# Gate signals of a fused GNN kernel given by a PE drain behind the last product instead of by the product

## The reference, cut to what matters

```python
def _lstm_last(seq, wih, whh, bih, bhh):
    ...
    def step(carry, x_t):
        h, c = carry
        g = x_t @ wih.T + h @ whh.T + b
        i, f, gg, o = jnp.split(g, 4, axis=-1)
        c = jax.nn.sigmoid(f) * c + jax.nn.sigmoid(i) * jnp.tanh(gg)
        h = jax.nn.sigmoid(o) * jnp.tanh(c)
        return ((h, c), None)
...
msgs = x[src].reshape(n, d, c)
aggr = _lstm_last(jnp.swapaxes(msgs, 0, 1), wih, whh, bih, bhh)
return aggr @ wl.T + bl + x @ wr.T
...
x = _layernorm(x + sage(relu(sage(x))))        # two layers of _sage_conv
h = jax.ops.segment_sum((x @ weight[rel])[src] * norm[:, None], dst, num_segments=512)
x = _layernorm(x + relu(h))
```

## Time and profile before

| | us |
|---|---|
| median of 3 executions | 535.96 |
| lowest and highest of them | 535.65, 536.25 |
| span of the profiled execution | 570.4 |
| busy in that span: PE | 485.2 (85%) |
| busy: PE weight loads (they overlap PE) | 349.4 (61%) |
| busy: DVE | 399.5 (70%) |
| busy: ACT | 325.8 (57%) |
| busy: POOL | 309.4 (54%) |

### The profile page before, as it was taken

One profiled execution on the slowest core, in us unless ns is written; L12 is line 12 of the kernel. 1 busy time (PEld: TensorE's weight loads), 2 busy tenths in 40 slices (PEclk: granted clock), 3 DMA queues, 4 the chain that ended last, 5 costly groups with the idle time before them and its releaser, 6 DMA issues.

```text
span 570.4 us, 9783 instructions
## 1 busy us (share of the span) xinstructions
PE 485.2 (85%) x3463; PEld 349.4 (61%) x3463; DVE 399.5 (70%) x1114; ACT 325.8 (57%) x832; POOL 309.4 (54%) x320
## 2 busy tenths in 40 slices
PE   8766998979897999778897888887899987978795
PEld 4644786757676785656666766775785543444343
DVE  5544887858676895557776776876787975757665
ACT  4734766737556674545565665655675664545543
POOL 6476565665546501676664566666204655656551
PEclk9997999979999999978989999999999999999899
DMA  5665665675646502665665456556202111111111
GB/s 191 204 188 168 180 192 159 177 195 161 175 125 197 166 11 93 187 180 161 172 169 148 134 163 183 167 169 181 77 1 79 48 38 38 42 38 41 39 42 29
DMA packets 28346, 72.85 MB, mean 128 GB/s; under 512 B 6795, under 2 KB 10691, under 8 KB 28298
## 3 DMA queue, kind: packets, MB, share of 16 engines
q0 software_dynamic: 20768, 64.77, 40.0%
q1 hardware_dynamic: 6442, 6.54, 4.0%
q10 hardware_dynamic: 1088, 0.92, 0.5%
HBM read 69.05 MB, written 3.16 MB: 127 GB/s over the span
## 4 chain that ended last, share of the span: by engine, by line
PE 39%; DVE 17%; ACT 16%; another core or an unknown queue 13%; issue 8%; DMA 6%; POOL 1%; DVEq 0%; ACTq 0%; POOLq 0%
PE gates L1254 18%; DMA edge_rows<-msg_table,msg_index 6%; PE gates L1247 5%; PE work L1254 4%; DVE msg_full L1090 3%; ACT act_if L601 3%; ACT h_hi L597 3%; DVE prod_fc L906 2%; DVE prod_ig L908 2%; ACT msg_full L750 2%; PE work L1247 2%; DVE h_full L877 2%; ACT act_o L619 2%; ACT tanh_c L593 2%
## 5 line engine op out<-in xcount | busy, mean ns | idle before, releaser
L524 POOL DMA_INDIRECT rows<-gate_table,src_steps x226 | 224.7, 994 | 165.1 <-issue 64.5
L1247 PE MATMUL gates<-ident,rows 128*128 128x128 f32 x686 | 99.5, 281 | 39.5 <-issue 20.8
L601 ACT ACTIVATE act_if<-gates 128x512 f32<-128x512 f32 x113 | 67.8, 600 | 104.1 <-remote 54.5
L539 POOL DMA_INDIRECT edge_rows<-msg_table,msg_index x76 | 75.5, 993 | 79.6 <-DMA msg_table<-table_sb 30.9
L1254 PE MATMUL gates<-h_hi,whh_hi 128*128 128x256 f16 x396 | 104.7, 283 | 13.1 <-ACT h_hi L597 6.6
L906 DVE TENSOR_TENSOR prod_fc<-act_if,cell 128x256 f32<-128x256 f32 x128 | 54.2, 424 | 81.3 <-issue 37.3
L1247 PEld LDWEIGHTS gates<-ident,rows 128*128 128x128 f32 x686 | 78.1, 144 | 52.1 <-issue 49.7
L1254 PE MATMUL gates<-h_hi,whh_lo 128*128 128x256 f16 x396 | 104.1, 281 | 0.0
L1254 PE MATMUL gates<-h_lo,whh_hi 128*128 128x256 f16 x396 | 88.1, 282 | 0.4 <-issue 0.4
L890 DVE TENSOR_TENSOR h_lo<-h_full,h_hi 128x256 f16<-128x256 f32 x128 | 54.2, 423 | 12.3 <-ACT h_hi L597 0.9
L1080 DVE TENSOR_SCALAR rows<-node_iota,dst_f 128x512 f16<-128x512 f16 x132 | 43.4, 365 | 26.8 <-ACT msg_full L750 25.7
(11 more groups left out here) (186 smaller groups left out, 800.5 us busy)
## 6 DMA issues: line engine op xcount, KB each, us to landing
rows<-gate_table,src_steps POOLq DMA_INDIRECT x226
gate_table<-rows SPq DMA_DIRECT2D x8, 256.0 KB
edge_rows<-msg_table,msg_index POOLq DMA_INDIRECT x76
code<-code_table SPq DMA_DIRECT2D x6, 160.0 KB
msg_table<-table_sb SPq DMA_DIRECT2D x4, 192.0 KB, 2.4
code<-code_table SPq DMA_DIRECT2D x5, 128.0 KB
whhT<-turned_whh SPq DMA_DIRECT2D x2, 256.0 KB
wihT<-turned_wih ACTq DMA_DIRECT2D x1, 256.0 KB, 2.9
```

Source lines behind the costliest of these rows:

```text
L524: pool.indirect_dma_start(rows[:, j * K + k, :], None, gate_table[l], bass.IndirectOffsetOnAxis(src_steps[:, t, k:k + 1], axis=0)).then_in ...
L539: pool.indirect_dma_start(edge_rows[:, c % 2, n, :], None, msg_rows, bass.IndirectOffsetOnAxis(msg_index[:, pool_first(c) + n:pool_first(c ...
L601: act.activation(act_if[:, h, :], gates[:, h, 0, :], ACT.Sigmoid, scale=1 / G_SCALE).then_inc(if_ready[h], 1)
L1247: pe.matmul(gate_place(t, h, gate)[:, k * P:(k + 1) * P], rows[:, j * K + 2 * h + k, gate * P:(gate + 1) * P], ident[:, :], is_transpose=True,
```

## The change

The method `then_inc` is taken off the last product of each group and put on a `pe.drain()` that is added behind it. The semaphores, their counts and those who wait for them stay as they were. `drain` is an instruction of PE's sequencer. All of it lies in `recurrent`; the first step of each layer (`first_gates`) and step 1 of the first layer (`picked_last`) keep their signals on the matmuls.

```diff
                     pe.wait_ge(h_lo_ready[h], split)
-                    products(t, h, BANKS[0], (hi,), h_lo, True).then_inc(gates0[h], 1)
+                    products(t, h, BANKS[0], (hi,), h_lo, True)
+                    pe.drain().then_inc(gates0[h], 1)
                     if apart(t):
                         products(t, h, (GATE_G,), (hi, lo), h_hi)
-                        products(t, h, (GATE_G,), (hi,), h_lo, True).then_inc(gates1[h], 1)
+                        products(t, h, (GATE_G,), (hi,), h_lo, True)
+                        pe.drain().then_inc(gates1[h], 1)
                         products(t, h, (GATE_O,), (hi, lo), h_hi)
-                        products(t, h, (GATE_O,), (hi,), h_lo, True).then_inc(gates_o[h], 1)
+                        products(t, h, (GATE_O,), (hi,), h_lo, True)
+                        pe.drain().then_inc(gates_o[h], 1)
                     else:
                         products(t, h, BANKS[1], (hi, lo), h_hi)
-                        products(t, h, BANKS[1], (hi,), h_lo, True).then_inc(gates1[h], 1)
+                        products(t, h, BANKS[1], (hi,), h_lo, True)
+                        pe.drain().then_inc(gates1[h], 1)
```

## The result

The changed kernel takes 580.68 us (median of 4 executions, 579.02 to 581.35), the kernel before 535.81 (535.04 to 536.25): a ratio of 1.0856, 95% interval 1.0815 to 1.0898, slower by 45 us.

What follows compares the result with a forecast made beforehand. PE's throughput was taken to bound an undisturbed step, going from 4.43 to 6.21 us. Over 58 steps that gave 103 us, plus 6 for five other steps, less 5: +104 on 535.96, 640 us, range 592 to 672.

Steps and rivals of the forecast that it cites:

- the two loops: In a step with six drains, PE's own work was put at 6.21 us, the loop of dependences at 5.38 us.
- the closing drain: PE's drain at the kernel's end, taken to end 0.32 us behind the start of PE's last matmul.
- 0.30 us for each drain: PE's loss at each drain: 0.27 us between products, and with the slower second matmul 0.30 us.
- the long waits add: ACT's long waits at PE's signals, 54.5 us in 20, were to stay on top of the drains' cost; chance 0.55.
- The rival that swallows the waits: Long waits pass while PE works through its drains: 591 to 614 us; chance 0.24, shared with a cheap restart.
- don't become late: POOL's gathers wait for `gates1[1]` and come later, but their slot is read that much later too; no cost.
- the 5 us taken off: Six steps with one-hot selections (t = 2, 12, 21, both layers) hide half 0's three stalls, about 0.9 us each.
- The dearer drain: Each drain costs 0.10 us more than its row says: +37 us, 677 us; chance 0.12.
- the cheap restart: Matmuls behind a drain are taken in at once, losing 0.21 us: 609 us; chance 0.24, shared with swallowed waits.
- the drain that holds nothing: A drain gives only its signal, each step later by 0.05 us: +3 us, 539 us; chance 0.03.
- The clock: PE's clock falls to 1.2 GHz in the gaps, a step takes 10.5 us: +354 us, about 890 us; chance 0.03.
- Faster by freed signals: The sequencer's signal avoids the products' late way and ACT's waits shrink, at most 20 us: 519 us; chance 0.01.

Runs made afterwards that it cites:

- the run with signals on the products: Changed kernel with its drains kept but the signals put back on the last products, as before the change: 586.0 us.
- the pair without gathers: Kernel before and changed kernel, each with only the first 20 of 226 gathers: 485.7 us and 581.86 us.
- the second profile: Kernel before, unchanged, in a second profiled execution: 536.69 us, with a span of 534.9 us.
- the first profile: Kernel before, unchanged, in the profiled execution that the prediction read: span 570.4 us, where plain executions took 535.81 us.

## Why the prediction was wrong

**Right: what bounds an undisturbed step, and that a drain holds PE.** 40 matmuls at 0.109 us, each drain holding all products behind it, and PE the longer of the two loops: all as worked out. An undisturbed step was forecast at 6.21 us and takes 6.05.

**Nearly right: the price of a drain.** Forecast 0.38 us from product to product and 0.03 for the slower second one, 0.30 in all. Measured 0.354, and 0.117 instead of 0.109 for the second, so 0.25. The restart of 0.06 us, taken from the restart behind a sequencer wait, was exact. The 0.32 us before it were not: they came from the closing drain. The matmul ahead of it carries a signal, and the run with signals on the products has 0.320 us too; that this is the whole reason isn't shown, since that matmul has another shape. The signal reaches ACT 0.33 us behind the product's start (413.36 against 413.03) instead of 0.31, where 0.05 us more was forecast. The second matmul's 0.03 us belongs to transposes of 32-bit rows (0.136 us behind the sixth drain), products pay 0.008. Behind the sixth drain I put 0.05 us for the sequencer's wait; it is 0.15 (0.502 against 0.354). Summed: 5 x 0.245 + 0.393 + 5 x 0.008 + 0.027 = 1.69, and 4.36 + 1.69 = 6.05. The undisturbed cost by this is 58 x 1.62 = 94 us, and the pair without gathers differs by 96. The step "0.30 us for each drain" was a tenth too high.

**Wrong: that the long waits add.** This is the step that failed: "So I take them as additive". Its ground was that the waits arise at PE's own signals, where drains can't hide them. In executions like the second profile there are no such late signals. The steps' long waits there are 52 us in which PE waits for rows, and gathers go on while PE stands at a drain, so the drains' time came out of these waits: the 58 steps grew by 36.5 us, where 103 were forecast.

The rival that swallows the waits had the right form, for another reason. Its lower end, each step the longer of 6.21 us and its old length, was given as +49 us; worked out again from the starts of `tanh_c` it is +48 on the first profile and +47 on the second, so the unusual profile did it no harm. With 6.05 instead of 6.21 it is +40. The rest to 36.5 is a balance: steps that were longer than 6.05 us lost waits too, and those with one-hot selections now last longer than 6.05. So its 591 to 614 was too high mainly by the price of a drain.

The sentence that gathers come later and "don't become late" looked in one direction only: it asked whether drains delay the gathers, not whether the gathers were what the steps waited for. In the first profile they weren't: late signals had slowed PE so far that the rows lay ready, as the distances above show. The 35.5 us between the two spans lie ahead of t = 3 (16.2), in the 58 steps (10.3) and between the layers (9.9), less 1.0 behind. So the average step of the first profile, 5.78 us, was near the 5.60 of the second by coincidence: one kind of wait stood in the place of another.

**Right by luck: the 5 us taken off.** They were put to the six steps with one-hot selections. In the pair without gathers the 58 steps do lack 6 us to 58 x 1.62, but 4.5 of them are at t = 3 to 6 of the first layer, and no step with a one-hot selection grew by more than 0.2 us less than 1.62.

**Where the 96 us went.** From before (second profile) to after, by the starts of `tanh_c`: ahead of t = 3 30.8 to 33.5 us; the 58 steps 324.8 to 361.3; between the layers 30.6 + 3.0; the stages behind 148.6 to 150.3. In sum +44 in the span. Without gathers on either side the 58 steps grow from 273.1 to 361.1, by 88; with them they grew by 36.5, because 324.8 - 273.1 = 52 us of waiting for rows were in them and are not in the drained kernel. In that, no first transpose starts less than 0.76 us behind the landing of its rows, and the median is 17 us.

**The other rivals.** The dearer drain, the cheap restart and the drain that holds nothing are refuted by 0.354 us from product to product. The clock didn't fall to its lower level: it was granted at 0.993 over the changed kernel's span, with gaps of 0.08 us behind five drains of a step and 0.23 behind the sixth. Faster by freed signals: the plain pace had none to free.

**A sign that was there.** The profiled span was 34.4 us longer than the plain executions, and I took that as waits which "may belong to the profiled execution alone" and left the sum on them. Every other profile of this case has a span within 3 us of its kernel's median. A profile that disagrees with the executions by 6% should have been used for durations of instructions only, and the pace of the steps should have been estimated from the gathers too. Four gathers of 262 KB each are 1.05 MB, and at the 206 GB/s of 35 to 40 us, a stretch in which PE hardly worked, that is 5.1 us, more than 4.43. POOL's issues alone, 0.95 us and 0.30 to the next, make 5.0 us of four. (The 162 GB/s from 30 to 213 us of that profile says less: the gathers were held up there by PE's late steps.)

## What to carry to other kernels

A cost on an engine that isn't what paces the loop is paid only as far as it goes beyond that pace, so find out what paces it before adding up, and ask of each wait what it would be if that one resource were free: leaving a resource's work out in one run showed at once what both the gathers (50 us) and the drains (96 us) are worth, and that they overlap. A signal belongs on the matmul: a drain in its place lets nothing start until the last matmul is done, and costs 0.25 us where products follow and 0.4 us where sequencer waits do. And compare a profile's span with the plain executions first: it was 34.4 us off in the misleading one and within 3 us in all others here. When they disagree like that, take another profile.

## What the runs showed of the hardware

A drain of PE ends 0.294 us after the start of a 256-column matmul, and the next matmul starts 0.060 us later. If the last matmul raises a semaphore itself, the drain ends 0.025 us later (0.320 against 0.294). Where the sequencer's waits and a transpose follow, it is 0.502 us from start to start.

Three indirect gathers of 128 rows of 2 KB in flight brought four of them in about 5.6 us; a fourth in flight gave 44 us over 226 gathers, a fifth some 8 more, and eight no more that can be told. The median from issue to landing stayed at 3.7 to 3.8 us throughout. How much of the old pace was bytes and how much the latency of a single gather stays open: with half the rows 20 of 50 us were left, with four in flight 8.

One recorded execution showed PE's signals late while PE worked on, as in the earlier trace rows, where ACT started 3.75 us behind the product instead of 0.31, and its span was 35.5 us longer than the second profile of the same kernel. What did that is open; it didn't come back in that second profile, nor in any other run here.
